# Attention over pairs of heads, with the value products in batches and in two column halves

## The reference

```python
kqv = (x @ Wqkv + bqkv).reshape(b, s, 3, 16, 32)
q, k, v = kqv[:, :, 0], kqv[:, :, 1], kqv[:, :, 2]
scores = einsum('bsnh,btnh->bnst', k, q) / sqrt(32)
scores = triu(scores) + -10000.0 * tril(ones, k=-1)
attn = softmax(scores, axis=2)
out = einsum('bnkq,bknh->bqnh', attn, v).reshape(b, s, 512)
out = out @ Wo + bo
...
w = _FP4_LUT[nibbles] * scale      # gate, up and down weights of the FFN
```

## Time and profile before

| | |
|---|---|
| median of 3 runs | 2273.49 us (2268.86 to 2274.01) |
| profiled execution, span from first to last instruction | 2264.3 us |
| the profiled execution's own time | the page gives its span alone |
| mean granted clock of TensorE | 0.954 |
| attention stage with score and value units | 189.5 to 760.6 us, 571.1 us |
| PE / DVE / ACT / POOL busy in the span | 2045.9 / 1102.0 / 701.9 / 552.3 us |

### The profile page before, as it was taken

The page is one execution under the profiler, slowest core; times in us unless marked ns, Lnnn a source line. Parts: engine busy times, 40 slices in busy tenths (PEclk is TensorE's granted clock), DMA queues, the critical chain, the costliest instruction groups (busy, mean ns, idle before and its releaser), DMA issues. The chain is left out here.

```text
span 2264.3 us, 26630 instructions
## 1 busy us (share of the span) xinstructions
PE 2045.9 (90%) x8097; PEld 1341.5 (59%) x8097; DVE 1102.0 (49%) x2138; ACT 701.9 (31%) x1312; POOL 552.3 (24%) x650
## 2 busy tenths in 40 slices
PE   6988999999999979999997889999788888888787
PEld 5874444444444568787785667777455565555554
DVE  5426666666567622322325846778333333333332
ACT  2212455554445311212212332221222332222222
POOL 2003333333335400000003513111222222222222
PEclk9997999999999989999998999999899999999898
DMA  6333333333332152000002002003688778877885
GB/s 218 124 124 101 116 112 107 108 121 112 109 118 80 51 203 104 1 1 1 1 1 91 1 6 88 33 24 112 208 284 265 258 251 282 271 244 256 284 258 150
DMA packets 125975, 298.68 MB, mean 132 GB/s; under 512 B 18576, under 2 KB 29328, under 8 KB 125648
## 3 DMA queue, kind: packets, MB, share of 16 engines
q1 hardware_dynamic: 111568, 262.10, 32.7%
q0 software_dynamic: 14336, 35.66, 7.7%
HBM read 228.46 MB, written 68.98 MB: 131 GB/s over the span
## 5 line engine op out<-in xcount | busy, mean ns | idle before, releaser
L732 PE MATMUL bank<-probs,v_ones 128*64 128x512 f32 (+3 forms) x768 | 330.4, 512 | 0.0
L834 DVE TENSOR_REDUCE max_parts<-bank 128x1 f32<-128x512 f32 (+3 forms) x384 | 211.8, 556 | 188.5 <-PE bank L708 108.7
L806 ACT ACTIVATE probs<-bank 128x512 f32<-128x512 f32 (+3 forms) x384 | 188.5, 491 | 279.7 <-PE bank L720 208.5
L1736 POOL DMA_INDIRECT out_x<-e_y,row_out x64 | 101.5, 1586 | 478.0 <-ACT e_y L1794 474.0
L1772 PE MATMUL bank<-w_gate,xgt 128*128 128x352 f32 x512 | 206.7, 559 | 0.0
L705 PEld LDWEIGHTS bank<-k_stack,q_stack 96*128 96x128 f32 x384 | 75.3, 196 | 207.2 <-DVE max_parts L834 148.7
L705 PE MATMUL bank<-k_stack,q_stack 96*128 96x512 f32 (+3 forms) x384 | 173.3, 459 | 7.2 <-DMA k_stack<-qk_parts 7.1
L1840 DVE TENSOR_TENSOR e_hidden<-e_silu,bank 128x352 f32<-128x352 f32 x64 | 33.4, 521 | 267.6 <-issue 215.2
L1772 PE MATMUL bank<-w_up,xgt 128*128 128x352 f32 x512 | 162.3, 460 | 0.0
L234 PE MATMUL bank<-ln_xt_hi,gu_hi 128*128 128x512 f32 x352 | 141.8, 403 | 15.8 <-DMA gu_lo<-fp_out 11.1
L717 PE MATMUL bank<-q_stack,k_stack 98*128 98x512 f32 (+3 forms) x384 | 153.5, 400 | 0.0
(11 more groups left out here) (238 smaller groups left out, 4150.1 us busy)
## 6 DMA issues: line engine op xcount, KB each, us to landing
w_gate<-in_w_gate SPq DMA_DIRECT2D x64, 704.0 KB, 5.9
w_up<-in_w_up SPq DMA_DIRECT2D x64, 704.0 KB, 7.8
w_down<-in_w_down SPq DMA_DIRECT2D x64, 512.0 KB, 8.2
q_stack<-qk_parts SPq DMA_DIRECT2D x96, 128.0 KB, 2.5
k_stack<-qk_parts SPq DMA_DIRECT2D x96, 128.0 KB, 2.8
w_down<-in_w_down SPq DMA_DIRECT2D x64, 192.0 KB, 8.9
fp_words<-in_fp_words SPq DMA_DIRECT2D x32, 264.0 KB, 2.7
fp_out<-fp_w SPq DMA_DIRECT2D x32, 264.0 KB
```

What stands on the lines that cost most here:

```text
L732: pe.matmul(m.bank[OUTB[c]][0:2 * HD, q0 - c * CH:q0 - c * CH + n], vs[u][:, k, :], probs[i % EXPS][:, 0:n], start=(k == 0), stop=(k == (c ...
L806: act.activation(probs[i % EXPS][:, 0:n], m.bank[EXPB[i % 3]][:, 0:n], ACT.Exp, scale=scale).then_inc(exp_ready, 1)
L834: dve.tensor_reduce(parts[u % 2][:, half, q:q + 1], m.bank[MAXB[i % 3]][:, 0:n], AX.X, ALU.max).then_inc(max_part_ready, 1)
L1736: pool.indirect_dma_start(out=a["out"][:, :], out_offset=bass.IndirectOffsetOnAxis(ap=row_out[u][:, :], axis=0), in_=y[u % 2][:, :], in_of ...
```

## The change

The attention now goes over 16 pairs of heads. A pair has 24 units of each kind, in which the two heads take turns, and 4 rounds. In a round PE does six exp units, in the first three rounds with eight max units of the next pair between them, and then the six value units of the round before as one batch (`value_round`). `probs` has twelve buffers for that. The second head's value product goes to rows 64 to 127 of the bank, so it uses the other half of the array's columns. The stacks are three slots of two heads. The maxima of a pair are turned together into a bank of the max units, copied by DVE, and placed by four DMAs; they are one pair ahead, where they were two heads ahead.

ACT copies whole banks (four head parts in 128 rows) into `out_pair`. DMAs take the output rows to their place in `attn`, and the two rows of sums as 128 x 16 into `sums`; DVE inverts these 16 columns, a DMA stores them to memory, two more read them back spread over 32 rows each, and POOL multiplies 128 x 1024 once for four heads. The loops are written out in full. The FP4 expansion uses two DVE steps (shift up, arithmetic shift down, then a bit mask, which gives a float16 pattern), one multiplication on POOL, and a factor in the high and the low step; the value itself is no longer stored.

```diff
+    def vector_bits(self, dve, n):
+        if n == 0:
             dve.wait_ge(self.shift_ready, 2)
-        b = u % 2
-        dve.wait_ge(self.loaded[b], 32 * (2 * g + u // 2 + 1))
-        need(dve, self.nibbles_used, h)
-        dve.tensor_scalar(self.bits[:, :], self.words[b][:, :], self.shift[:, :], 7, ALU.logical_shift_right,
-                          ALU.bitwise_and).then_inc(self.nibbles_ready, 1)
-    def vector_signs(self, dve, u):
-        b = u % 2
-        dve.tensor_scalar(self.sign[:, :], self.words[b][:, :], self.shift3[:, :], 1, ALU.logical_shift_right,
-                          ALU.bitwise_and).then_inc(self.nibbles_ready, 1)
-    def vector_codes(self, dve, h):
-        dve.wait_ge(self.nibbles_ready, 3 * h + 1)
-        dve.scalar_tensor_tensor(out=self.codes[:, :], in0=self.bits[:, :], scalar=4.0, in1=self.bits[:, :],
-                                 op0=ALU.max, op1=ALU.add).then_inc(self.nibbles_ready, 1)
-    def gpsimd_values(self, pool, h, u):
-        STEPS = 4
-        done = 0
-        def then(instruction):
-            nonlocal done
-            done += 1
-            instruction.then_inc(self.step, 1)
-            wait_apart(pool, self.step, h * STEPS + done, self.index_ready)
-        wait_apart(pool, self.nibbles_ready, 3 * (h + 1), self.index_ready)
-        then(pool.tensor_scalar(self.bent[:, :], self.codes[:, :], 12.0, -16.0, ALU.max, ALU.add))
-        then(pool.tensor_tensor(self.codes[:, :], self.codes[:, :], self.bent[:, :], ALU.add))
-        then(pool.tensor_scalar(self.bent[:, :], self.sign[:, :], -1.0, 0.5, ALU.mult, ALU.add))
-        then(pool.tensor_tensor(self.bent[:, :], self.bent[:, :], self.scales[u % 2][:, :], ALU.mult))
-        need(pool, self.stored, 48 * h)
-        pool.tensor_tensor(self.w[:, :], self.codes[:, :], self.bent[:, :], ALU.mult).then_inc(self.nibbles_used, 1)
-    def scalar_hi(self, act, h):
-        act.wait_ge(self.nibbles_used, h + 1)
-        need(act, self.stored, 48 * h)
-        act.activation(self.hi[:, :], self.w[:, :], ACT.Copy).then_inc(self.hi_ready, 1)
-    def vector_lo(self, dve, h):
-        dve.wait_ge(self.hi_ready, h + 1)
-        dve.tensor_tensor(self.lo[:, :], self.w[:, :], self.hi[:, :].bitcast(F32), ALU.subtract).then_inc(self.w_ready, 1)
-    def sync_store(self, sp, h):
-        sp.wait_ge(self.w_ready, h + 1)
-        cols = bass.ds(h * SLICE, SLICE)
-        for n, t in enumerate((self.w, self.hi, self.lo)):
-            sp.dma_start(self.a["fp4_out"][n, :, cols], t[:, :].bitcast(F32)).then_inc(self.stored, 16)
+        dve.wait_ge(self.loaded[n % 2], 32 * (n // 2 + 1))
+        need(dve, self.bits_ready, n)
+        dve.tensor_scalar(self.spread[:, :], self.words[n % 2][:, :], self.shift[:, :], 19, ALU.logical_shift_left,
+                          ALU.arith_shift_right).then_inc(self.spread_ready, 1)
+        dve.wait_ge(self.spread_ready, n + 1)
+        need(dve, self.scaled_ready, n)
+        dve.tensor_scalar(self.bits[:, :], self.spread[:, :], 0x8E00, 0, ALU.bitwise_and,
+                          ALU.bitwise_or).then_inc(self.bits_ready, 1)
+    def gpsimd_scale(self, pool, n):
+        pool.wait_ge(self.bits_ready, n + 1)
+        need(pool, self.lo_ready, n)
+        halves = self.bits[:, :].bitcast(F16).rearrange("p (n t) -> p n t", t=2)
+        pool.tensor_tensor(self.scaled[:, :], halves[:, :, 0], self.scales[n % 2][:, :], ALU.mult).then_inc(self.scaled_ready, 1)
+    def scalar_hi(self, act, n):
+        act.wait_ge(self.scaled_ready, n + 1)
+        need(act, self.stored, 32 * n)
+        act.activation(self.hi[:, :], self.scaled[:, :], ACT.Copy, scale=self.TO_VALUE).then_inc(self.hi_ready, 1)
+    def vector_lo(self, dve, n):
+        dve.wait_ge(self.hi_ready, n + 1)
+        dve.scalar_tensor_tensor(out=self.lo[:, :], in0=self.scaled[:, :], scalar=self.TO_VALUE,
+                                 in1=self.hi[:, :].bitcast(F32), op0=ALU.mult, op1=ALU.subtract).then_inc(self.lo_ready, 1)
+    def sync_store(self, sp, n):
+        sp.wait_ge(self.lo_ready, n + 1)
+        cols = slice(n * SLICE, (n + 1) * SLICE)
+        for part, t in enumerate((self.hi, self.lo)):
+            sp.dma_start(self.a["fp4_out"][part, :, cols], t[:, :].bitcast(F32)).then_inc(self.stored, 16)
...
-    SLOTS = 4
-    AHEAD = 2
+    PAIRS = HEADS // 2
+    GROUPS = HEADS // 4
+    SLOTS = 3
...
-    LAG = 3
-    LAST0 = max(i for i, (k, q0, n) in enumerate(EXP_UNITS) if q0 < CH)
+    assert N == len(EXP_UNITS) == 12
+    U = 2 * N
+    ROUNDS = 4
+    EXP_ROUND, MAX_ROUND = U // ROUNDS, U // (ROUNDS - 1)
+    FIRST_DONE = 2 * TPC
     MAXB, EXPB, OUTB = (0, 1, 7), (2, 3, 4), (5, 6)
-    TURNED = (OUTB[0], slice(2 * HD, 2 * HD + 2 * QT))
-    EXPS = 6
+    PROBS = 2 * EXP_ROUND
...
+            def place_max(p):
+                slot = p % SLOTS
+                sp.wait_ge(max_copied, p + 1)
+                for j in range(2):
+                    for half in range(2):
+                        row = (2 * j + half) * QT
+                        sp.dma_start(qs[slot][j][ROWS + half:ROWS + half + 1, :].rearrange("a (t c) -> a t c", c=P).bitcast(F32),
+                                     top_t[p % 2][row:row + QT, :].bitcast(F32)).then_inc(max_placed[slot], 16)
+            def move_out(p):
+                sp.wait_ge(out_copied, 2 * (p + 1))
+                sp.wait_ge(v_placed, 2 * min(PAIRS, (p // 2 + 1) * 2))
+                need(sp, inverted, p)
+                for j in range(2):
+                    rows = slice((2 * j + 1) * HD, (2 * j + 1) * HD + 1)
+                    sp.dma_start(sums[j * S // 16:(j + 1) * S // 16, :],
+                                 out_pair[p % 2][rows, :].rearrange("a (q c) -> a q c", c=16)).then_inc(sums_loaded, 16)
+                for j in range(2):
+                    u = (2 * p + j) % 4
+                    sp.dma_start(m.attn[u * HD:(u + 1) * HD, p // 2, :],
+                                 out_pair[p % 2][2 * j * HD:(2 * j + 1) * HD, :]).then_inc(out_placed, 16)
+            def store_inverse(p):
+                sp.wait_ge(inverted, p + 1)
+                sp.dma_start(a["sums"][p].rearrange("(q c) -> q c", c=16), inverse[:, :]).then_inc(inverse_stored, 16)
+            def spread_inverse(p):
+                sp.wait_ge(inverse_stored, 16 * (p + 1))
+                if p == 0:
+                    sp.wait_ge(wo_ready, 1)
+                need(sp, normalized, p // 2 - 1)
+                for j in range(2):
+                    u = (2 * p + j) % 4
+                    sp.dma_start(spread[p // 2 % 2][u * HD:(u + 1) * HD, :],
+                                 a["sums"][p, j * S:(j + 1) * S].partition_broadcast(HD)).then_inc(inverse_spread, 16)
...
+            for p in range(SLOTS):
+                load(p)
+            dq.sync_load(sp, 0)
             sp.dma_start(wo_raw[:, :, :], a["wo"].rearrange("(k p) n -> p k n", p=P)).then_inc(wo_loaded, 16)
-            dq.sync_load(sp, 0, 0)
-            for u in range(AHEAD):
-                place_max(u, u)
-            over_heads(sp, step)
-            dq.sync_store(sp, HEADS - 1)
-            sp.wait_ge(dq.stored, 48 * HEADS)
+            place_max(0)
+            for p in range(PAIRS):
+                if p >= 1 and p + 2 < PAIRS:
+                    sp.wait_ge(scored, U * p)
+                    load(p + 2)
+                dq.sync_load(sp, 2 * p + 1)
+                if p >= 1:
+                    dq.sync_store(sp, 2 * p - 1)
+                    move_out(p - 1)
+                if p + 1 < PAIRS:
+                    dq.sync_load(sp, 2 * p + 2)
+                    place_max(p + 1)
+                dq.sync_store(sp, 2 * p)
+                if p >= 1:
+                    store_inverse(p - 1)
+                    spread_inverse(p - 1)
...
+            def normalize(g):
+                pool.wait_ge(out_placed, 64 * (g + 1))
+                pool.wait_ge(inverse_spread, 64 * (g + 1))
+                pool.tensor_tensor(m.attn[:, g, :], m.attn[:, g, :], spread[g % 2][:, :], ALU.mult).then_inc(normalized, 1)
...
-                pe.matmul(m.bank[OUTB[c]][0:2 * HD, q0 - c * CH:q0 - c * CH + n], vs[u][:, k, :], probs[i % EXPS][:, 0:n],
-                          start=(k == 0), stop=(k == (c + 1) * TPC - 1)).then_inc(weighed, 1)
...
+                pe.wait_ge(exp_ready, u + 1)
+                pe.matmul(m.bank[OUTB[c]][j * 2 * HD:(j + 1) * 2 * HD, q0 - c * CH:q0 - c * CH + cols], vs[p % 2][j][:, k, :],
+                          probs[u % PROBS][:, 0:cols], start=(k == 0), stop=(k == (c + 1) * TPC - 1)).then_inc(weighed, 1)
...
+            for p in range(PAIRS):
+                for r in range(ROUNDS):
+                    ahead = MAX_ROUND if r < ROUNDS - 1 and p + 1 < PAIRS else 0
+                    scored_ahead = 0
+                    for n in range(EXP_ROUND):
+                        exp_unit(p, EXP_ROUND * r + n)
+                        while scored_ahead < ahead * (n + 1) // EXP_ROUND:
```

(54 more changed lines are left out.)

362 lines of the change are left out of this document (146 added, 216 removed).

## The result

The changed kernel took 2072.36 us (median of four runs, 2071.13 to 2072.98) against 2271.18 us (four runs, 2268.34 to 2274.01): a ratio of 0.9134, interval 0.9114 to 0.9155. The span of its profile is 2070.1 us, 194.2 less than before.

The account below looks back on a forecast made before the run. PE bounds the attention stage (571 us). 5 + 15 x 25.6 + 19 = 408 us, so -163, and -5 at the end: 2273.5 less 168 is 2106 us; own range 2070 to 2145, wider range 2068 to 2195.

Parts of the forecast that it names:

- two streams side by side: Value products of different column halves run at once: 9216 columns a pair take 7.7 us in place of 15.4.
- rival 1: The column halves take turns and only the batching counts: -91 us, 2182 us; chance 0.19.
- The entry: PE's way into a value unit from score products: some 0.2 us each, twenty a pair removed, -4.0 us.
- The way of the maxima: Pair's end, FP4 steps to landing: 8.7 us against PE's 7.2, so 1.5 waiting, and about 0.5 in the third round.
- The restarts: Each of a pair's four rounds restarts engines that have run dry: at worst 2 us a pair, all charged.
- Twelve transfers: Stage start: pair 0 needs twelve stack transfers where head 0 needed six, 3.7 us; with 1.5 for queued maxima, +5.
- the last term: The last pair, with no maxima to compute: 19 us including restarts.
- The end, for which I had -5: Behind the last pair, six pieces of normalizing leave DVE, for which PE waited 4.37 us and more: -5 us.
- stay below 21.1: DVE at 18.0 us and ACT at 14.2 us a pair stay under PE's 21.1, so their savings alone are worth nothing.
- The signs: Expected profile: a pair in 24 to 28 us, PE under 95% busy, waits at first exp unit, reciprocals under 10 us.
- a drain at each change of half: PE empties itself whenever the column half changes, so nothing overlaps: slower, 2310 us; chance 0.06.
- The end of the pair: Halves overlap, but late maxima or FP4 words make each pair 3 to 5 us longer: 2165 us; chance 0.07.

Follow-up runs that it names:

- the one-half kernel: The changed kernel with both heads' value products written to rows 0 to 63, so one column half, the two heads summed: 2185.38 us, ratio 0.9624.
- the batches of two: The changed kernel with value units in batches of two behind every second exp unit, 12 batches a pair in place of 4: 2192.99 us, widely scattered.

## Why the prediction was right, and where its size was off

**The halves.** The step that I was least sure of, two streams side by side, held exactly: 0.83 ns a column against 1.67, 8.41 us a pair for values and exits where I had 7.7 and 0.6. My estimate of 1.6 times from the Trainium skill, "TensorE: Matmul & The Clock Gate", Part 3, was too low: the ratio here is 2.0 a column, 1.9 with the constant. That rows and halves go together leaves one thing open: whether the overlap comes from separate columns of the array or from separate result rows no run here can tell. What the Trainium skill states in "TensorEngine Tiling (Array Packing)", Key Properties, that tiles work independently, the trace bears out: 2.80 us for 3072 columns in two halves, 5.29 in one.

**The batching.** Right as a sum: 85 us against the 91 of rival 1, whose time of 2182 the one-half kernel met at 2185. A pair there takes 30.7 us against my 29.4 and one of restarts. The entry was too dear at 0.2: the score part of a pair is 14.4 us, and not 12.1 + 4 x 0.2 + 0.4 = 13.3. If the exits are right, 20 entries were worth 2.9 us, 0.14 each. The 17.85 us a head, from which the 12.1 came, was also a mean over all 32 heads; in the middle a head took 17.99 (485.64 us for 27), which makes it 0.15.

**The wait at a pair's end.** The way of the maxima is 8.4 us, as I had it (8.7), but PE has 7.9 us of work and a wait of 0.27 beside it and not 7.2. The wait is 0.28 us in place of 1.5, and the third round's 0.5 did not show; 0.27 stands in the fourth, where ACT is behind.

**The restarts.** This is the step that failed: 2 us a pair for engines that have run dry are nothing. Waits of the changed kernel from 190 to 560 us (us in total, times, longest):

```profile
PEld bank L736 <- issue: 36.7, 150, 0.6
PEld bank L721 <- DMA q_stack<-neg_max_t: 22.5, 16, 4.8
PEld bank L721 <- ACT probs L781: 13.2, 27, 0.8
PEld bank L701 <- DVE max_parts L821: 3.1, 14, 0.2
```

A reduction does start late after a batch, but PE has three banks ahead and waits for DVE 3.1 us in all. I had charged the idle start of an engine that nobody was waiting for. So 8.3 + 13.3 + 2.0 + 2.0 = 25.6 became 8.4 + 14.4 + 0.55 + 0 = 23.35: 15 x 2.25 = 34 us. It lies just under my lower bound of 23.5. That 34 is also the whole distance from 2106 is chance, since the terms below nearly cancel. The 2072 is also in my own range of 2070 to 2145 by rounding alone: 23.5 us a pair, 15 x 2.1 below 2106, is 2074.5.

**Start, last pair, end.** Twelve transfers delay PE's first product by 1.5 us, not 5, and the first exp unit by 0.4, since before it also stood behind the second head's maxima (turned at 188.68). The stage from 189.5 to 564.7 is 0.4 + 15 x 23.35 + 24.6; I had 19 for the last term. The last pair itself takes 19.8 us (544.87 to 564.7), so that term was right to 0.8. The other 4.5 or so are the first pair's, 27.8 us (189.92 to 217.76) at first at the granted clock of 0.50 (the lower level, 1.2 GHz). Its first 13.3 us of exp and max units are 7.9 in the middle (4.16 and 3.74), and its first batch takes 0.58 longer (2.66 against 2.08); the 1.44 us of a batch that it does not have go off. I had not looked at the clock at the start, where the kernel before has the lower clock too, but for 7.5 us of its stage and not for 15. The end, for which I had -5: up to the experts -3.2, then +4.8 in the experts' stage, which is within its scatter. Together 2096 - 34 - 4.6 + 5.6 + 6.6 is 2070, the span that was measured. The 9.2 us between span and median, which I carried over, are 2.3 here: the profiled execution of before was itself some 7 us shorter than the median of its timed ones.

**The fed engines.** That their savings are worth nothing by themselves was right for FP4 (0.9987). That both "stay below 21.1" was too easy a test. VectorE has about 15.6 us a pair (226.53 in 338) where I had 18.0; with the old 5.4 it would be at 21 of 23.35, and yet that costs 48 us, and in three rounds it binds with no more work at all. So the work that left VectorE was worth a quarter of the gain, if it would have stood in the first two rounds, where I put it. The fourth round has no reductions and VectorE is idle there for 4 us (401.2 to 405.3); what the old work would cost there no run shows.

**The signs.** The reciprocals came to 3.9 us in all, and PE does wait at the first exp unit of a pair. But a pair took 23.35 us and not 24 to 28, and PE was busy for 365.20 of 375.20 us, 97%, and not under 95%. The stages behind are 1.6 us longer, within the 2 that I gave them, only because -3.2 and +4.8 meet.

**Rivals.** Turns and a drain at each change of half are both excluded by the one-half kernel and the batches of two. The end of the pair never binds by more than 0.3 us.

## What to carry to other kernels

When an fp32 product uses 64 weight columns and there are two independent ones, put their outputs in the two column halves and alternate them in the code: the columns then cost half, even in batches of two, and up to two units' distance still overlaps. Take border costs between kinds of product from a kernel that only batches them, and do not charge a start-up of an engine that has buffers between it and the bound one. Check a fed engine by the round in which its work stands, and not by the mean over a period, and look at the granted clock behind new waits of PE: in two experiments waits of 0.2 to 0.5 us were followed by some 3 us at half clock. And judge the last 10 us of this kernel by a stage, or by runs on one chip, since the experts' stage alone scatters by 16.

## What the runs showed that I had not expected

- Two fp32 products in different column halves overlap fully: 0.83 ns a column for both together, with 1.67 in one half.
- The overlap reaches across up to four matmuls (two units) of the other half that stand ahead, but not across six: 1.66 us saved in a batch of 3072 columns where 2.5 were possible.
- Where PE had waits that the changed kernel doesn't have, the granted clock fell to 0.50 for a while: with batches of two for long stretches, with the old work on VectorE for 3.3 us in every pair, with three rounds for 3.5 us in half of the pairs. In the middle of the changed kernel it stays at 1.00. What exactly brings it down stays open.
